# State-space chunks of a hybrid kernel: state in four quarters, B and C as one operand, D on ScalarE, two gate buffers

## What is computed

```python
zxbcdt = u @ in_w.T
z, xBC, dt = jnp.split(zxbcdt, [D_INNER, D_INNER + CONV_DIM], axis=-1)
dt = softplus(dt + dt_bias)
xBC = silu(causal_depthwise_conv4(xBC) + conv_b)
xh, Bm, Cm = jnp.split(xBC, [D_INNER, D_INNER + D_STATE], axis=-1)
state = exp(dt * A) * state + (dt * x_t)[..., None] * B_t
y_t = einsum('bhpn,bn->bhp', state, C_t) + D * x_t
y = y * silu(z)
y = y * rsqrt(mean(y * y) + EPS) * rms_w
out = y @ out_w.T
```

## Time and profile before

| | us |
|---|---|
| median of 3 runs | 1596.35 |
| lowest and highest run | 1593.54, 1597.09 |
| the profiled execution | 1584.21 |
| its span (first to last instruction) | 1582.5 |
| busy in the span: PE | 1282.2 (81%) |
| busy: DVE | 1056.0 (67%) |
| busy: ACT | 750.2 (47%) |
| busy: POOL | 350.4 (22%) |
| chain that ended last: PE | 49% |
| chain: DVE | 22% |
| chain: issue | 12% |

### The profile page before, as it was taken

One profiled execution on the slowest core, in us unless ns is written; L12 is line 12 of the kernel. 1 busy time (PEld: TensorE's weight loads), 2 busy tenths in 40 slices (PEclk: granted clock), 3 DMA queues, 4 the chain that ended last, 5 costly groups with the idle time before them and its releaser, 6 DMA issues.

```text
span 1582.5 us, 34281 instructions
## 1 busy us (share of the span) xinstructions
PE 1282.2 (81%) x12654; PEld 886.8 (56%) x12655; DVE 1056.0 (67%) x1666; ACT 750.2 (47%) x1158; POOL 350.4 (22%) x360
## 2 busy tenths in 40 slices
PE   3725699998548999974739999865999999999996
PEld 2215576675347676642324555453677777777674
DVE  3666778888567888876976766664547774757431
ACT  2228456555465655631255234241546674546431
POOL 0112234444313453440220000006301001101010
PEclk9757799999779999996959999955999999999998
DMA  8043000000310000004021000036736663636111
GB/s 284 12 146 113 8 3 2 1 1 1 114 60 2 3 1 1 2 20 194 1 90 54 0 0 0 1 110 245 215 126 223 209 206 98 239 126 226 34 27 20
DMA packets 36072, 127.43 MB, mean 81 GB/s; under 512 B 8568, under 2 KB 10408, under 8 KB 26032
## 3 DMA queue, kind: packets, MB, share of 16 engines
q1 hardware_dynamic: 27568, 104.06, 18.4%
q0 software_dynamic: 8448, 22.62, 5.3%
HBM read 105.54 MB, written 21.14 MB: 80 GB/s over the span
## 4 chain that ended last, share of the span: by engine, by line
PE 49%; DVE 22%; issue 12%; ACT 6%; POOL 5%; DMA 4%; DVEq 0%; POOLq 0%; SPq 0%; ACTq 0%
PE banks L2125 14%; PE banks L2146 14%; DVE mb_ca L607 6%; PE banks L1663 4%; PE banks L1693 3%; PE banks L975 2%; PE banks L999 2%; POOL mb_ysq L903 1%; POOL xs_table L2158 1%; POOL mb_ring L926 1%; POOL mb_quad L931 1%; DVE mb_S L676 1%; PE banks L340 1%; PE banks L1068 1%; DVE sq L260 1%
## 5 line engine op out<-in xcount | busy, mean ns | idle before, releaser
L2125 PE MATMUL banks<-eb_x_hi,eb_w_hi 128*128 128x128 f16 x1344 | 228.8, 220 | 2.0 <-DVE eb_x_lo L2025 2.0
L2125 PE MATMUL banks<-eb_x_lo,eb_w_hi 128*128 128x128 f16 x1344 | 228.7, 220 | 0.0
L2125 PE MATMUL banks<-eb_x_hi,eb_w_lo 128*128 128x128 f16 x1344 | 228.7, 220 | 0.0
L975 PE MATMUL banks<-mb_u_hi,mb_wi_hi 128*128 (+3 forms) x1152 | 203.9, 222 | 29.5 <-ACT mb_sz L830 15.4
L975 PE MATMUL banks<-mb_u_hi,mb_wi_lo 128*128 (+3 forms) x1152 | 203.5, 222 | 0.0
L975 PE MATMUL banks<-mb_u_lo,mb_wi_hi 128*128 (+3 forms) x1152 | 203.3, 221 | 0.0
L607 DVE SCALAR_TENSOR_TENSOR mb_ca<-mb_xp,mb_par,mb_ca 128x128 f32<-128x128 f32 x384 | 159.4, 478 | 6.0 <-ACT mb_ca L799 3.9
L975 PEld LDWEIGHTS banks<-mb_u_hi,mb_wi_hi 128*128 128x128 f16 (+1 forms) x1152 | 113.9, 99 | 47.4 <-issue 46.0
L2125 PEld LDWEIGHTS banks<-eb_x_hi,eb_w_hi 128*128 128x128 f16 x1344 | 132.3, 98 | 4.7 <-issue 2.4
L2125 PEld LDWEIGHTS banks<-eb_x_lo,eb_w_hi 128*128 128x128 f16 x1344 | 132.3, 98 | 2.4
L2125 PEld LDWEIGHTS banks<-eb_x_hi,eb_w_lo 128*128 128x128 f16 x1344 | 132.4, 98 | 0.0
(11 more groups left out here) (437 smaller groups left out, 3095.8 us busy)
## 6 DMA issues: line engine op xcount, KB each, us to landing
eb_raw<-e_w SPq DMA_DIRECT2D x36, 1024.0 KB, 5.4
eb_un<-e_w SPq DMA_DIRECT2D x28, 1024.0 KB, 8.1
mb_ring<-m_in_w SPq DMA_DIRECT2D x8, 1072.0 KB, 5.2
xs_table<-zero POOLq DMA_DIRECT2D x1, 6400.0 KB, 20.3
eb_xg<-xs_table POOLq DMA_DIRECT2D x23, 256.0 KB, 2.9
ab_raw<-a_in_w SPq DMA_DIRECT2D x4, 1154.0 KB, 12.6
mb_ring<-m_out_w SPq DMA_DIRECT2D x4, 1024.0 KB, 5.1
xcm<-x_cm SPq DMA_DIRECT2D x4, 512.0 KB, 5.2
```

Of the source, the lines that this page charges most:

```text
L975: x = e.matmul(ps[0:width, bank, n * P:(n + 1) * P], a[:, k, f:f + width], b[:, k, ds(i * P, P)], start=(k == 0 and m == 0), stop=(k == KD ...
L2125: o = e.matmul(ps[:, j, c * P:(c + 1) * P], a[:, side, k, f * P:(f + 1) * P], b[:, k, :], start=(k == 0 and m == 0), stop=(k == KD - 1 and ...
```

## The change

- The state S is held as [128, 256]: partitions 32q to 32q + 31 hold the 32 state rows of channel quarter q. `faded` gets a tile of its own of that shape. The increment is written by four matmuls into four groups of partitions; the product with C becomes two matmuls of 512 columns against `cdiag`, a [128, 4, 128] tile that is zero except for C at (q, q).
- B and C are one operand of 64 partitions: one projection, one evacuation, one convolution of 128 columns, one SiLU. SP copies the C half into the four diagonal places of `cdiag` by DMA, for each chunk after `bcc_done`. PE waits for the first copy (`c0_in`) before the B-C product and for the other three (`c_in`) before the product with the state.
- D times x moves from POOL to ACT (`skip`, after `grow`).
- The gate has two buffers (`sz[:, side]`), and `project_z` no longer waits for `y_done`. The chunk loop is unrolled by two so that the side is known.
- The SiLU of B and C moves between the two SiLUs of x.
- On DVE `next_state` and `row_stats` move into the second half of the convolution, behind `from_state`.
- On POOL `conv_bc` moves ahead of `power`; `ring_free` is raised in the first chunk instead of the last. The exponential that makes `edec` is done in four pieces. The parameters of the B/C convolution are laid out for 64 partitions.

```diff
-    edec, dte = sb("edec", [P, TT, H2]), sb("dte", [P, TT, H2])
+    edec, dte = sb("edec", [P, TT, H2 // 4]), sb("dte", [P, TT, H2])
...
-    sz = sb("sz", [P, JD, P])
...
+    xc, bcc = sb("xc", [P, JD, P]), sb("bcc", [2 * NS, P])
...
+    cdiag = sb("cdiag", [P, 4, P])
+    sz = sb("sz", [P, 2, JD, P])
...
-    S = sb("S", [NS, DI])
+    S, faded = sb("S", [P, DI // 4]), sb("faded", [P, DI // 4])
...
+        body(0, l * TT, True, False, 0)
+        with e.Fori(0, TT // 2 - 1) as r:
+            body(r * 2 + 1, l * TT + r * 2 + 1, False, False, 1)
+            body(r * 2 + 2, l * TT + r * 2 + 2, False, False, 0)
+        body(TT - 1, l * TT + TT - 1, False, True, 1)
...
+            def c_rows(g):
+                e.wait_ge(bcc_done, g + 1)
+                core.apart(e)
+                for q in range(4):
+                    e.dma_start(cdiag[q * NS:(q + 1) * NS, q, :], bcc[NS:2 * NS, :]).then_inc(c_in if q else c0_in, 16)
+
             pair_rows(0)
+            c_rows(l * TT)
...
                 pair_rows(i)
+                c_rows(l * TT + i)
...
-                    e.tensor_tensor(yi.rearrange("p j t -> p (j t)"), ps[:, 5:7, :].rearrange("p b n -> p (b n)"),
-                                    ec.rearrange("p j t -> p (j t)"), ALU.mult).then_inc(yi_done, 1)
+                    e.tensor_tensor(by_half(yi), ps[:, 5:7, :].rearrange("p h (q t) -> p h q t", q=4), by_half(ec), ALU.mult)\
...
-                    e.tensor_tensor(S[:], faded, ps[0:NS, 3:5, :].rearrange("p b n -> p (b n)"), ALU.add).then_inc(s_done, 1)
+                    e.tensor_tensor(S[:], faded[:], ps[:, 3, 0:DI // 4], ALU.add).then_inc(s_done, 1)
...
                 def last_rows():
                     if not is_first:
                         add_rows(i - 1, g - 1)
                     from_state()
+                    next_state()
+                    if not is_first:
+                        row_stats(i - 1, g - 1)
...
-                next_state()
...
                 e.wait_ge(sz_done, 2 * (g + 1))
-                e.tensor_tensor(y, y, sz[:], ALU.mult).then_inc(y_done, 1)
-                if not is_first:
-                    row_stats(i - 1, g - 1)
+                e.tensor_tensor(y, y, sz[:, side, :, :], ALU.mult).then_inc(y_done, 1)
...
-                own(e.activation(edec[:], ps[:, 3, TT * H2:2 * TT * H2].rearrange("p (i h) -> p i h", i=TT), ACT.Exp))
+                for q in range(4):
+                    rows = slice(q * NS, (q + 1) * NS)
+                    x = e.activation(edec[rows, :, :], ps[rows, 3, TT * H2:2 * TT * H2].rearrange("p (i h) -> p i h", i=TT)
+                                     [:, :, q * 8:q * 8 + 8], ACT.Exp)
+                own(x)
...
+            def skip(g):
+                e.wait_ge(xc_done, 2 * (g + 1))
+                for j in range(JD):
+                    x = e.activation(dx[:, j, :], xc[:, j, :], ACT.Copy, scale=par[:, MB_DCOL + j:MB_DCOL + j + 1])
+                x.then_inc(dx_done, 1)
...
-                e.activation(bcp[:, :, 3:P + 3], ps[0:NS, 0, 0:2 * P].rearrange("p (c t) -> p c t", c=2), ACT.Copy)
+                e.activation(bcp[:, 3:P + 3], ps[0:2 * NS, 0, 0:P], ACT.Copy)
                 if not is_first:
                     e.wait_ge(bcc_done, g)
-                for c in range(2):
-                    w = MB_BCW + 4 * c + TAPS - 1
-                    x = e.activation(cbc[:, c, :], ps[0:NS, 0, c * P:(c + 1) * P], ACT.Identity,
-                                     scale=par[0:NS, w:w + 1], bias=par[0:NS, MB_BCB + c:MB_BCB + c + 1])
-                x.then_inc(bc_ev, 1)
+                w = MB_BCW + TAPS - 1
+                e.activation(cbc[:], ps[0:2 * NS, 0, 0:P], ACT.Identity,
+                             scale=par[0:2 * NS, w:w + 1], bias=par[0:2 * NS, MB_BCB:MB_BCB + 1]).then_inc(bc_ev, 1)
                 if is_first:
...
                 else:
                     grow(g - 1)
+                    skip(g - 1)
                     e.wait_ge(xtr, g)
...
-                e.wait_ge(acc_bc, g + 1)
-                if not is_first:
-                    e.wait_ge(inter_mm, g)
-                e.activation(bcc[:], cbc[:], ACT.Silu).then_inc(bcc_done, 1)
-
-            def project_z(g, is_first):
-                if not is_first:
-                    e.wait_ge(y_done, g)
+                    if q == 0:
+                        e.wait_ge(acc_bc, g + 1)
+                        if not is_first:
+                            e.wait_ge(inter_mm, g)
+                        e.activation(bcc[:], cbc[:], ACT.Silu).then_inc(bcc_done, 1)
+
+            def project_z(g, side):
                 for q in range(2):
                     e.wait_ge(z_mm, 2 * g + q + 1)
-                    e.activation(sz[:, 4 * q:4 * q + 4, :], ps[:, 1 - q, :].rearrange("p (j t) -> p j t", j=4),
+                    e.activation(sz[:, side, 4 * q:4 * q + 4, :], ps[:, 1 - q, :].rearrange("p (j t) -> p j t", j=4),
                                  ACT.Silu).then_inc(sz_done, 1)
...
+                    skip(g)
...
+                    project_z(g + 1, 1 - side)
...
-                w = par[0:NS, MB_BCW:MB_BCB].rearrange("p (c k) -> p c k", c=2)
-                part = [ysq[0:NS, 2 * k + 2:2 * k + 4, :] for k in range(TAPS - 1)]
                 for k in range(TAPS - 1):
-                    x = e.tensor_tensor(part[k], bcp[:, :, k:k + P], w[:, :, k].unsqueeze(2).to_broadcast([NS, 2, P]), ALU.mult)
+                    x = e.tensor_tensor(part[:, k, :], bcp[:, k:k + P],
+                                        par[0:2 * NS, MB_BCW + k:MB_BCW + k + 1].to_broadcast([2 * NS, P]), ALU.mult)
...
+            def body(i, g, is_first, is_last, side):
+                if is_first:
+                    e.wait_ge(w_lo, (l + 1) * MB_PIECES)
+                    core.apart(e)
+                    e.sem_inc(ring_free, 1)
+                else:
                     e.wait_ge(s_done, g)
                     core.apart(e)
-                e.tensor_tensor(heads(faded), heads(S[:]), edec[0:NS, i, :].unsqueeze(2).to_broadcast([NS, H2, 32]),
+                e.tensor_tensor(few_heads(faded[:]), few_heads(S[:]), edec[:, i, :].unsqueeze(2).to_broadcast([P, H2 // 4, 32]),
                                 ALU.mult).then_inc(smul, 1)
                 if not is_first:
                     sum_squares(g - 1)
-                e.wait_ge(xc_done, 2 * (g + 1))
-                e.tensor_tensor(dx, xc[:], par[:, MB_DCOL:MB_DCOL + JD].unsqueeze(2).to_broadcast([P, JD, P]), ALU.mult)\
-                    .then_inc(dx_done, 1)
+                if not is_last:
+                    conv_bc(g + 1)
                 if not is_first:
                     power(g - 1)
-                if not is_last:
-                    conv_bc(g + 1)
                 e.wait_ge(dx_done, g + 1)
                 e.wait_ge(yi_done, g + 1)
                 e.tensor_tensor(yi, yi, dx, ALU.add).then_inc(yid_done, 1)
-                if is_last:
-                    e.wait_ge(s_done, g + 1)
-                    core.apart(e)
-                    e.sem_inc(ring_free, 1)
-                else:
+                if not is_last:
                     keep_halo(g + 1)
 
...
-                project(i, 0, [MB_CB, MB_CC], NS, bc_mm)
+                project(i, 0, [MB_CB], 2 * NS, bc_mm)
...
-                e.wait_ge(bcc_done, g + 1)
+            def body(i, g, is_first, is_last, side):
+                e.wait_ge(c0_in, (g + 1) * 16)
...
-                e.transpose(ps[:, 2, 0:NS], bcc[:, 0, :], core.ident[0:NS, 0:NS])
-                e.matmul(ps[:, 2, P:2 * P], bcc[:, 0, :], bcc[:, 1, :], start=True, stop=True).then_inc(g_mm, 1)
+                e.transpose(ps[:, 2, 0:NS], bcc[0:NS, :], core.ident[0:NS, 0:NS])
+                e.matmul(ps[:, 2, P:2 * P], bcc[0:NS, :], cdiag[0:NS, 0, :], start=True, stop=True).then_inc(g_mm, 1)
...
-                for j in range(JD):
-                    x = e.matmul(ps[:, 5 + j // 4, (j % 4) * P:(j % 4 + 1) * P], S[:, j * P:(j + 1) * P], bcc[:, 1, :],
+                e.wait_ge(c_in, (g + 1) * 48)
+                core.apart(e)
+                for half in range(2):
+                    x = e.matmul(ps[:, 5 + half, :], S[:, half * P:(half + 1) * P], cdiag[:].rearrange("p q t -> p (q t)"),
                                  start=True, stop=True)
                 x.then_inc(inter_mm, 1)
                 e.wait_ge(ec_done, g + 1)
-                for q in range(2):
-                    x = e.matmul(ps[0:NS, 3 + q, :], btok[:], xe[:, q * 512:(q + 1) * 512], start=True, stop=True)
+                for q in range(4):
+                    x = e.matmul(ps[q * NS:(q + 1) * NS, 3, 0:DI // 4], btok[:], xe[:, q * (DI // 4):(q + 1) * (DI // 4)],
+                                 start=True, stop=True)
                 x.then_inc(ds_mm, 1)
                 if is_first:
```

(18 more changed lines are left out.)

41 lines of the change are left out of this document (19 added, 22 removed).

## The result

The changed kernel takes **1551.45 us** (median of 4 runs, 1548.04 to 1553.89), the kernel before, on the same chip, 1596.72 us (4 runs, 1593.54 to 1597.51). The ratio is 0.972, 95% interval 0.9706 to 0.9734: 45.3 us less. The prediction said 1559.0 us, range 1545 to 1582.

The account below looks back on a forecast made before the run. A loop through several engines, none full, bounds the kernel. Middle chunks go from 30.18 to 14.6 + 12.8 = 27.4 us; with layer ends 18.4 a layer, 37 off 1596.35 gives 1559 us, range 1545 to 1582.

Parts of the forecast that it names:

- The loop and the wait for sz: No engine is full; PE stands 1.40 us before the x projection for the gate, which waits for DVE's multiply.
- A to B: From PE's x projection start to DVE's row_norm start: 15.30 us becomes 14.6, the halved B/C projection saving 0.72.
- B to intra: From row_norm's start on DVE to PE's intra-chunk product: 3.3 us, after add_rows, which waits for GpSimd's power, ends at 3.2.
- ds in 0.5 us: State increment on PE: eight records to four column groups overlap, 0.51 us instead of 1.76.
- rival 2: The state increment's matmuls do not overlap: intra starts 0.6 us later a chunk, 1567 us; chance 0.10.
- State update, decay, multiply: DVE's update 1.20 to 0.42 us, GpSimd's decay 1.90 to about 0.73, DVE's multiply by the gate 2.02 to 1.22.
- D on ScalarE: Eight ACTIVATEs taking 3.0 us, or 2.3 by the skill's estimate; GpSimd's yi + dx no later, nothing gained directly.
- Copies of C: SP's copies before PE's B/C product: 2.1 us to landing plus 0.3 issue, hidden by 4.0 us of cover.
- Rival 4: The change does not reach the loop; another wait, such as a late C copy, holds the x projection: 1596 us, chance 0.03.
- Rivals 1 and 3, the lock: GpSimd's conv_bc holds DVE's taps: 1580 us, chance 0.15; or it also keeps its length, no tap passing: 1609 us, 0.07.
- rival 3: conv_bc keeps 4.4 us, no tap passes; slower once add_rows ends over 6.0 us after row_norm's start: 1609 us, chance 0.07.
- better, 3.5 a chunk: No stall of DVE under conv_bc, add_rows ending 2.5 us after row_norm's start: 1549 us, chance 0.03.

Follow-up runs that it names:

- the first two experiments: Kernel before with only two gate buffers: 1579.21 us, ratio 0.9907; changed kernel with one gate buffer again: 1561.2 us, 0.9785.

## Why the prediction was right, point by point

**The loop and the wait for sz: right.** The wait for the single gate buffer is confirmed by the first two experiments: it went with the second buffer (1.98 us a chunk) and part of it came back without it (0.83). What was late next was PE, as said, but with a small wait before intra.

**A to B: 14.21 us, predicted 14.6.** The B/C projection fell from 1.43 to 0.76 us, as worked out. The sum left out 0.41 us, the slow first block behind a stop. The stretch is shorter as said, but that the saved 0.72 us is worth 0.72 us of the period, as the sum had it, was wrong: it took PE for the bound up to intra, and with conv_bc ahead of power PE was not. Doing the work again cost nothing. This is the step of the prediction that failed. It did not spoil the total, because terms that the sum had left out or taken too long were worth more: the slow first block, and the shorter z and products (below). That is luck.

**B to intra: 3.27 us, predicted 3.3.** add_rows ends at 526.41, B + 3.2, exactly the value taken. conv_bc spans 3.1 us (2.75 taken, gaps between its instructions were left out) and power ends at B + 2.27 (1.9 taken). The prediction priced this wait but did not see that it came from a part of the change that had better been left out. It had the row for that: power with conv_bc behind it ended 0.8 us after row_norm had started.

**ds in 0.5 us: right.** From start to start 0.49 us (0.51 taken); rival 2 falls. The product with the old state took 525.25 - 523.39 = 1.86 us (1.76 taken). But in the changed kernel PE then stood 0.57 us before intra, so the gain did not reach the period whole. No run takes the state in quarters out by itself, so its worth is argued from these rows. With power first the period is 28.20 - 25.89 = 2.31 us under that of the gate buffers alone; 0.67 of it is the B/C projection, and the 1.64 that is left is near the 1.26 + 0.11 of the two state products.

**State update, decay, multiply: right in size, off the path.** 0.41 us (0.42), 0.62 (0.73), 1.32 (1.22). That the update's new place is worth nothing was said, and its experiment shows it.

**D on ScalarE: right that it is worth nothing.** The eight took 2.43 us; the prediction's 3.0 was too long, and the estimate of 2.3 from the Trainium skill (ScalarE: Activation LUTs, the section on what ACT_TABLE_LOAD and an ACTIVATE cost) was the better one. dx was ready at B + 3.75 and waited for nothing.

**Copies of C: right**, 2.3 us against 4.7 at hand. Rival 4 falls.

**Rivals 1 and 3, the lock.** A tap is still held: the view of DVE's taps in the chunk gives min/median/max

```profile
L623 DVE SCALAR_TENSOR_TENSOR mb_ca<-mb_xp,mb_par,mb_ca x24: 339/347/1810, 519.3 to 531.8; 128x128 f32<-128x128 f32 x24
```

But conv_bc, 3.1 us long with 64 partitions and two gaps of 0.18 us, held DVE for only 0.42 us in the first half (3.91 against 3.49 us) and 0.50 in the tap round (1.79 against 1.29 with power first). In the run with B and C twice the tap round took 1.33 us, though the last two instructions of conv_bc ran beside it: there they held it by almost nothing. So the rule, taken strictly, does not fit the small instructions. The lock did not move over whole, and rival 3's place, with its threshold of B + 6.0, was missed by 2.8 us.

**The size of the gain: too low by 0.71 us a chunk.** A chunk gained 3.51 us, not 2.8: 1.09 between A and B (0.70 said; the 0.41 of the first block was left out) and 2.42 between B and A (2.08 said: B to intra 0.03 better than put, z 5.46 us instead of 5.66, the products behind it 1.84 instead of 1.98, intra 0.05 worse). The prediction had a case of that size, "better, 3.5 a chunk", and gave it 0.03, but not for this reason: that case had add_rows at B + 2.5, and it was at B + 3.2. Over the seven periods of each layer the traces give 27.6 and 25.1 us, 52.7 together; the prediction had 6 x 2.8 + 2.1 + 0.7 = 19.6 a layer, 39.2. The first layer gained 2.5 us more than the second because of its first chunk, 32.64 us before and 26.47 after: behind a wait of PE of 3.0 us in both kernels, the granted clock fell to the 1.2 GHz level, in the kernel before for some 10 us (first line, PEclk 0.51), in the changed kernel for some 3.4 (second line).

```profile
185.50:196.00 10.50, 10.50 (x80) 7.02 (x81) 9.89 (x21) 4.67 (x9) 6.45 (x7) 0.51 0.00 0
186.00:189.50 3.50, 3.50 (x11) 1.63 (x9) 3.43 (x11) 3.50 (x12) 1.97 (x5) 0.54 0.00 0
```

**The layer's ends gave part of it back, more than was said.** The first chunk begins 1.3 us later, well inside the spread: over all thirteen traces it begins between 168.1 and 174.1 us. The way from the last chunk of the first layer to the first of the second grew from 91.56 to 96.02 us, 4.5 more. 52.7 - 1.3 - 4.5 = 46.9 us up to the last chunk; 45.3 were timed. The prediction had 1.2 a layer, 2.4. Of the growth, some 1.3 us lie on the way to the second half of the output of the last chunk (0.9 said) and 0.5 in the exponent in four pieces (0.3 said). A larger part is one wait of DVE ahead of the layer's normalised input, first in the kernel before, then in the changed one:

```profile
421.62 0.20 DVE L570 RECIPROCAL mb_rstd<-mb_rstd 128x8 f32<-128x8 f32 x1 [0.53 <-ACT mb_rstd L757]
399.81 0.20 DVE L586 RECIPROCAL mb_rstd<-mb_rstd 128x8 f32<-128x8 f32 x1 [3.06 <-issue]
```

PE's wait for that input grew from 5.1 to 7.6 us. DVE stands there 3.06 to 3.33 us on "issue" in all twelve traces other than that of the kernel before, the gate buffers alone and the one gate buffer in the changed kernel among them. So it comes neither with the second gate buffer nor with the state or with B and C. The unrolled loop is in all twelve. But the trace of the kernel before is also the one that lacks the "issue" waits of PE in the expert block and lies 12.5 us under its kernel's median, so it is not shown that the change causes this wait at all. Over the twelve the way between the layers takes 93.4 to 96.8 us.

So the forecast of 37 us less holds two errors of opposite sign: 13.5 us too little for the chunks, of which some 3 are the clock in the first chunks, and 3.4 too little taken off for the ends. That makes the 46.9 us of the traces; 45.3 were timed.

## What to carry to other kernels

Read the loop from mark to mark and ask of each saving on the busiest engine whether that engine then only waits at the next meeting point: here a saved projection was worth 0.72 us on paper, nothing in one order of GpSimd's stream and 0.67 in another. When a change has many parts, price the ones that look like mere reordering as well; the one that put the longer work ahead of a 0.6 us instruction with a waiting reader cost about 10 us. Before a difference between two profiles is explained, look where each lies among its kernel's timed runs: the one of before was 12.5 us off. Where DVE reads two SBUF tiles, look for the GpSimd instruction that runs beside it before calling a duration work.
